# Row statistics on ACT, a split opening, a last tile in halves, and a POOL clip for ten weight tiles

## What is computed

```python
# stage 1: a gated mixer: per head, outer products of a context with itself,
# a causal convolution of 1024 taps, contracted with the normalised input
kv  = einsum('bhil,bhjl->bijhl', ctx, ctx)             # 64 heads, head_dim 8
y   = irfft(rfft(kv, 2 * L) * rfft(ssm_kernel, 2 * L))[..., :L]
out = einsum('bijhl,bhil->bjhl', y + kv * D, layernorm(x))
x   = x + tanh(g_xattn) * out
# stage 2: a gated feed-forward block with MXINT8 operands
h = bf16(layernorm(bf16(layernorm(x))) * ln_w + ln_b)
h = bf16(mx_quant(h) @ mx_quant(W1).T + b1)            # 1024 -> 4096
h = bf16(gelu_tanh(h))
h = bf16(mx_quant(h) @ mx_quant(W2).T + b2)            # 4096 -> 1024
x = x + tanh(g_ffn) * bf16(bf16(layernorm(x)) + h)
# mx_quant: blocks of 32, amax, scale = 2**floor(log2(amax)) / 64, round, clip to [-128, 127]
```

## Time and profile before

| | us |
|---|---|
| median of 3 runs | 1933.82 (1930.59 to 1935.32) |
| the profiled execution | 1932.06 |
| its span, first to last instruction | 1930.3 |
| PE busy in the span | 1854.4 (96%) |
| DVE busy | 1625.8 (84%) |
| ACT busy | 1042.8 (54%) |
| POOL busy | 880.8 (46%) |

### The profile page before, as it was taken

One profiled execution on the slowest core, in us unless ns is written; L12 is line 12 of the kernel. 1 busy time (PEld: TensorE's weight loads), 2 busy tenths in 40 slices (PEclk: granted clock), 3 DMA queues, 4 the chain that ended last, 5 costly groups with the idle time before them and its releaser, 6 DMA issues. The chain is left out here.

```text
span 1930.3 us, 28627 instructions
## 1 busy us (share of the span) xinstructions
PE 1854.4 (96%) x11432; PEld 1476.1 (76%) x11432; DVE 1625.8 (84%) x1866; ACT 1042.8 (54%) x1311; POOL 880.8 (46%) x645
## 2 busy tenths in 40 slices
PE   6999999999999989999987897999999999999998
PEld 5999889999998879998975566666667776666773
DVE  5888898989999979998859998988988888889843
ACT  5666656555668677776734345444454543444440
POOL 2888888788899889998940000000000000000000
PEclk9999999999999999999998998999999999999999
DMA  7665657777757587785758312112212212121112
GB/s 241 213 221 175 192 180 229 228 260 267 220 188 234 188 254 209 242 256 188 212 202 328 88 55 77 66 51 70 77 45 77 77 68 69 51 77 56 44 44 77
DMA packets 165477, 294.24 MB, mean 152 GB/s; under 512 B 106144, under 2 KB 106144, under 8 KB 157152
## 3 DMA queue, kind: packets, MB, share of 16 engines
q1 hardware_dynamic: 165344, 292.41, 46.9%
HBM read 222.05 MB, written 45.68 MB: 139 GB/s over the span
## 5 line engine op out<-in xcount | busy, mean ns | idle before, releaser
L372 PE MATMUL y_ps<-kk_hi,slab 128*128 128x352 f32 (+6 forms) x3328 | 882.9, 348 | 33.6 <-DMA slab<-taps_scratch 18.4
L372 PEld LDWEIGHTS y_ps<-kk_hi,slab 128*128 128x128 f32 x3328 | 598.3, 190 | 89.7 <-issue 26.2
L372 PE MATMUL y_ps<-kk_lo,slab 128*128 128x352 f32 (+6 forms) x1664 | 576.4, 346 | 0.0
L1073 PE MATMUL l_ps<-f_xq_T,w_rest 128*128 128x256 bf16 x3136 | 348.4, 273 | 7.8 <-DMA f_xq_T<-f_hq 6.3
L1073 PEld LDWEIGHTS l_ps<-f_xq_T,w_rest 128*128 128x128 bf16 x3136 | 307.3, 98 | 47.5 <-issue 6.7
L1136 ACT ACTIVATE arena<-l_ps,b_c 128x256 bf16<-128x256 f32 x496 | 207.2, 473 | 247.4 <-PE l_ps L1073 242.4
L854 POOL TENSOR_TENSOR terms<-terms 128x768 f32<-128x768 f32 x127 | 332.1, 2615 | 10.0
L372 PEld LDWEIGHTS y_ps<-kk_lo,slab 128*128 128x128 f32 x1664 | 315.5, 190 | 27.2
L1374 POOL TENSOR_TENSOR f_rstd<-f_var_eps,f_neg_half 128x1 f32<-128x1 f32 x28 | 15.3, 548 | 673.0 <-DVE f_var_eps L1194 673.0
L1091 PE MATMUL acc_ps<-raw_room,arena 128*128 128x512 bf16 x1024 | 226.2, 379 | 0.0
L1091 PE MATMUL acc_ps<-w_T,arena 128*128 128x512 bf16 x1024 | 226.2, 379 | 0.0
(11 more groups left out here) (147 smaller groups left out, 2298.3 us busy)
## 6 DMA issues: line engine op xcount, KB each, us to landing
slab<-taps_scratch SPq DMA_DIRECT2D x128, 512.0 KB, 4.9
arena<-in_w_m SPq DMA_DIRECT2D x32, 1024.0 KB, 7.0
arena<-x_scratch SPq DMA_DIRECT2D x60, 512.0 KB, 3.8
raw_room<-in_ctx_e SPq DMA_DIRECT2D x64, 384.0 KB, 3.4
arena<-in_w SPq DMA_DIRECT2D x22, 1024.0 KB, 6.9
x_tile<-in_x_t SPq DMA_DIRECT2D x32, 512.0 KB, 5.0
out_t<-arena SPq DMA_DIRECT2D x32, 512.0 KB, 2.6
w_scratch<-arena SPq DMA_DIRECT2D x22, 512.0 KB, 7.4
```

What stands on the lines that cost most here:

```text
L372: mm = nc.tensor.matmul(y_ps[:, at + begin - first:at + end - first], slab[s][:, half, d * P:(d + 1) * P], kk_part[s][:, begin - d * PAIR: ...
L1073: mm = nc.tensor.matmul(l1_ps[bank % L1_BANKS][:, a, :], w1_tile(b)[:, k, a * P:(a + 1) * P], inputs[:, k, :], start=(k == 0), stop=(k == ...
```

## The change

1. **Opening of stage 1.** The gate is loaded first and has its own semaphore. The taps are scaled straight into their high half, and the low half is one `scalar_tensor_tensor`. The two halves are stored, waited for and read back one by one; PE starts on the high half's slab and takes the low taps of the first stretch last. ACT makes `high_half(0)` ahead of the statistics of the first tile.
2. **Jobs of stage 1.** ACT clips a job between `squares` and `high_half`, no longer after `copy_k`; SP loads the next job into a slot right behind that slot's `store_job`, one head earlier than before.
3. **Order of the first banks.** `LAG` goes; group 1 uses tiles 4 and 5 at once, then one bank of group 1 for every second tile, and the last five at the end.
4. **Row statistics on ACT.** `first_statistics` and `second_statistics` leave DVE: each is two ACT passes with an accumulator (mean, then square about the mean) and a small third one. For tiles 4 to 7 they are placed among the banks and gelus of groups 1 and 2, afterwards behind `norm_again`. The second statistics use the loaded tile as scratch, so the next load waits for them instead of for `first_norm`.
5. **DVE's order** in groups 1 and 2: peaks come after the inputs, and three peaks of group 2 between its two inputs.
6. **POOL clips.** `weight_clip` of the ten tiles moves from DVE to POOL; the quantisation of the first of these tiles is not held behind the next tile's integers.
7. **Last tile in halves.** Layer 2 of tile 31 runs all of the first 512 columns, then the others; sums and store go by halves.

```diff
 # SP, stage 1 (the store of each half of the taps has its own semaphore)
-            sp.wait_ge(taps_stored, 32)
-            load_slab(0)
+            sp.wait_ge(taps_stored[0], 16)
+            load_half(0, 0)
+            sp.wait_ge(taps_stored[1], 16)
+            load_half(0, 1)
...
-                if h - 2 in quant_of and quant_of[h - 2] + 3 < JOBS - 1:
-                    load_job(quant_of[h - 2] + 3)
...
                 if h - 1 in quant_of:
                     store_job(quant_of[h - 1])
+                    if quant_of[h - 1] + 3 < JOBS - 1:
+                        load_job(quant_of[h - 1] + 3)
 # ACT, stage 1
             squares(0)
+            high_half(0)
             ln_stats(0)
-            high_half(0)
...
                     squares(h + 1)
+                    if h in quant_of:
+                        job_clip(quant_of[h])
                     high_half(h + 1)
...
-                if h in quant_of:
-                    job_clip(quant_of[h])
 # stage 2: PE's order of the first banks
-    for b in range(FILL, banks + LAG):
-        first_banks += [(0, b)] if b < banks else []
-        first_banks += [(1, b - LAG)] if b >= FILL + LAG else []
+    first_banks = [(g, b) for g in range(2) for b in range(FILL, KEPT)]
+    for b in range(KEPT, banks):
+        first_banks += [(0, b)]
+        first_banks += [(1, (b + KEPT) // 2)] if (b - KEPT) % 2 == 0 else []
+    first_banks += [(1, b) for b in range(banks) if b >= FILL and (1, b) not in first_banks]
 # stage 2, ACT (second_statistics is the same on n_bf, with xin as scratch)
+            def first_statistics(t):
+                i, u = t % GROUP, t - EARLY
+                x = xin[t % X_LOADS]
+                act.wait_ge(x1_loaded[u % X_LOADS], 16 * (u // X_LOADS + 1))
...
+                nc.scalar.activation(n_bf[i][:], x, ACT.Identity, scale=-1.0 / L, accum_out=neg_mean1[i][:]).then_inc(mean1, 1)
...
+                nc.scalar.activation(n_bf[i][:], x, ACT.Square, bias=neg_mean1[i][:], accum_out=spread1[:]).then_inc(sum1, 1)
...
+                nc.scalar.activation(var_eps1[i][:], spread1[:], ACT.Copy, scale=1.0 / L, bias=EPS).then_inc(var1, 1)
...
+                if (g, b) == (1, banks - 2):
+                    first_statistics(EARLY)
+            gelu(1, 0)
+            first_norm(EARLY)
+            gelu(1, 1)
+            second_statistics(EARLY)
+            first_statistics(EARLY + 1)
+            gelu(1, 2)
+            first_norm(EARLY + 1)
+            second_statistics(EARLY + 1)
+            gelu(1, 3)
 # stage 2, DVE
                 weight_ints(j)
-                if j > KEPT:
+                if j > KEPT + 1:
                     weight_quant(j - 1)
                 weight_scales(j)
-                weight_clip(j)
-                if j in (KEPT, 11):
-                    peak(0, 0 if j == KEPT else 1)
+                if j == KEPT:
+                    weight_quant(j)
+                if j in (8, 12):
+                    peak(0, j // 4 - 2)
 # stage 2, POOL
+            def weight_clip(j):
+                pool.wait_ge(w_scaled, j - KEPT + 1)
+                nc.gpsimd.tensor_scalar(wq[j % 2], wq[j % 2], 127.0, None, ALU.min).then_inc(ints_ready, 1)
+
+            for j in range(KEPT, W_TILES):
+                weight_clip(j)
 # stage 2, PE: the last tile's layer 2
+                if t == tiles - 1:
+                    c = part
+                    for k in range(HID // P):
+                        mm = nc.tensor.matmul(acc_ps[s][:, c * 512:(c + 1) * 512], hidden[g % 2][:, k, s * P:(s + 1) * P],
...
```

More of the change, by code:

```diff
@@ L368, in conv_stretch @@
                 deepest = (end - 1) // PAIR
-                for d in range(deepest + 1):
-                    begin = max(first, d * PAIR)
[L371 to L374, removed]
+                terms_of = ((0, kk_hi), (0, kk_lo), (1, kk_hi))
+                order = [(d, c) for d in range(deepest + 1) for c in range(3)]
+                if h == 0 and i == 0:
+                    order = [(d, c) for d, c in order if c < 2] + [(d, c) for d, c in order if c == 2]
+                for n, (d, c) in enumerate(order):
+                    half, kk_part = terms_of[c]
+                    begin = max(first, d * PAIR)
+                    if h == 0 and i == 0 and (d, c) == (0, 2):
+                        pe.wait_ge(slab_loaded[0], 16)
+                    mm = nc.tensor.matmul(y_ps[:, at + begin - first:at + end - first], slab[s][:, half, d * P:(d + 1) * P],
+                                          kk_part[s][:, begin - d * PAIR:end - d * PAIR],
+                                          start=(n == 0), stop=(n == len(order) - 1))
                 if i in (1, len(stretches) - 1):
@@ L1012, in store @@
             def store(t):
-                sp.wait_ge(out_ready, t + 1)
-                sp.dma_start(out_t[order(t)], xfin).then_inc(out_stored, 16)
+                halves = 2 if t == tiles - 1 else 1
+                for c in range(halves):
+                    part = slice(c * L // halves, (c + 1) * L // halves)
+                    sp.wait_ge(out_ready, t + 1 + c)
+                    sp.dma_start(out_t[order(t)][:, part], xfin[:, part]).then_inc(out_stored, 16)
             def load_layer2(j):
@@ L1050, in _ @@
                     reload(GROUP * (g - 1) + 1)
[L1051 removed]
+            sp.wait_ge(out_stored, 16 * (tiles + 1))
         @block.tensor
@@ L1345, in _ @@
                         quantise_input(GROUP * (g + 1) + s)
-                    if g >= 2 and s == 0:
+                    if 2 <= g <= groups and s == 0:
                         gated_sum(GROUP * (g - 2) + 1)
@@ L1350, in _ @@
                         gated_sum(0)
-                    if 1 <= g < groups:
+                    if 3 <= g < groups:
                         peak(g, s)
+                    if g == 2 and s == 0:
+                        for q in range(3):
+                            peak(g, q)
+                if g == 1:
+                    peak(g, 0)
+                    peak(g, 1)
                 if g < groups:
-                    peak(g, 2)
+                    if g != 2:
+                        peak(g, 2)
                     peak(g, 3)
@@ L1357, in _ @@
                     hidden_quantise(g)
-                for s in range(GROUP):
-                    if g + 2 < groups:
-                        first_statistics(GROUP * (g + 2) + s)
                 if 2 <= g <= groups:
@@ L1386, in _ @@
             for g in range(2, groups):
-                for i in range(GROUP):
-                    first_rstd(GROUP * g + i)
-                for i in range(GROUP):
-                    second_rstd(GROUP * g + i)
+                if g < 4:
+                    for i in range(GROUP):
+                        first_rstd(GROUP * g + i)
+                        second_rstd(GROUP * g + i)
+                else:
+                    for i in range(GROUP):
+                        first_rstd(GROUP * g + i)
+                    for i in range(GROUP):
+                        second_rstd(GROUP * g + i)
 def gated_layer(nc, x_t, ctx_e, g_x, g_f, taps_in, skip_in, ln_w, ln_b, w1_t, w2_t, w_m, b1, b2, out_t):
```

150 lines of the change are left out of this document (86 added, 64 removed).

## The result

| | before | after |
|---|---|---|
| median, us | 1932.46 (4 runs) | 1944.34 (4 runs, 1943.13 to 1944.89) |
| ratio, 95% interval | | 1.0059 [1.0042, 1.0077] |
| profiled execution: span, us | 1930.3 | 1943.1 |
| stage 2 begins (its first matmul) | 1005.05 | 994.85 |
| last weight tile quantised, Q | 1053.74 | 1076.63 |

The account below looks back on a forecast made before the run. PE was taken as the bound wherever it has work. Terms of -2.8, -9, -6 and -1.5 summed to -19.3 us on 1932.1, giving 1912.8, or 1914.5 as median against 1933.8; range 1901 to 1936.

Parts of the forecast that it names:

- Part 3: Stage 2's ten weight tiles: with the clip on POOL a tile takes 5.5 us instead of 4.08, ten of them 14 more.
- X: POOL's price for clipping one weight tile, taken as 2.0 us, with 1.8 and 4.6 kept as other values.
- Rival A: Weight tiles: POOL's clip costs as much as two inputs, 4.6 us; 1940.5 us, slower than before; chance 0.17.
- the turns: Weight tiles: POOL and DVE alternate by whole instructions, so the clip's full price is added to DVE's pace.
- rival B: Weight tiles: POOL's clip costs 3.2 us, between forecast and two-input price; +12, so 1926.5 us; chance 0.15.
- the forecast's own slope: Weight tiles: for each us by which POOL's clip price is over 2.0, add 10 us.
- Part 4: Stage 2 after the weight tiles: new order pays their delay back, net -6 us at 1202, where PE becomes full.
- Parts 1 and 2: Stage 1: earlier opening, -2.8 us (0 to -3.4); earlier job loads remove two long PE waits, -9 us (0 to -12).
- Parts 5 and 6: Steady groups of stage 2: ACT's added statistics cost 0; last tile by halves: -1.5 us (-1.2 to -2).
- Rival C: Weight tiles: POOL and DVE do not exclude each other; a tile takes 3.5 us, Q is 1047, total 1897; chance 0.05.

Follow-up runs that it names:

- experiment 5: Changed kernel plus extra instructions behind its last sums: POOL clips and products alone, then POOL's clip beside short DVE passes; POOL's clip costs 2.53 ns an element and 0.2 us.
- experiment 6: Changed kernel plus POOL-alone instructions of 1024 columns behind its last sums, in several forms; tensor_scalar by min took 2.77 us.
- experiment 3: Changed kernel with POOL clipping only the first 1024 of each weight tile's 2048 columns: 1917.16 us, ratio 0.9923 to the kernel before.
- experiment 4: Changed kernel with the quantisation of groups 1 and 2 in four parts each, clip still on POOL: 1938.60 us, ratio 1.0037 to the kernel before.
- experiment 1: Changed kernel with the clip of the ten weight tiles back on DVE: 1904.08 us, ratio 0.9853 to the kernel before.

## Why the prediction was wrong

**The step that failed is Part 3, the price X of a clip on POOL.** It was taken as 2.0 us from a row of 128 elements, with 4.6 as the upper bound from the rows with two inputs. It is 5.36, above both ends. The 128-element row is an affine select, another form; `tensor_scalar` takes 0.53 us for as many. The bound rested on a tacit assumption, that one input can't cost more than two; experiments 5 and 6 show that on POOL it does: 2.77 us for 1024 elements of bf16 against 2.12. The nearest row in size and inputs was not near in form, and the range was cut at a bound with no reason for it. Rival A (X = 4.6, chance 0.17) came nearest with 1940.5 us, 4 below the measurement. That is partly luck: its price was still 0.76 us too low, and its turn as much too long as the forecast's. Its limit, slower from X = 3.9 on, lies between the two that were run: with half a clip, 2.77 us, the kernel was faster than before (experiment 3), with 5.36 slower.

The Trainium skill (GPSIMD Engine Reference, Elementwise - side-by-side cycle accounting) gives about 2.6 cycles an element for two inputs and 1.8 as the best case; rival B used the latter. At the 1.2 GHz that the page names, two float32 inputs come to 2.17 ns x 1.2 = 2.6 cycles, as it says, two bf16 inputs to (2114 - 190) / 1024 x 1.2 = 2.3, and `tensor_scalar` to 2.53 x 1.2 = 3.0, above both figures. The measurement decides.

**In the same part, the turns were sized too long.** The exclusion is real (experiment 5), but a two-input pass of DVE is held only for the clip less 1.8 us. POOL's addition of stage 1, on which the turns were read, had held DVE to 0.15 us before its end (647.68 + 3.75 - 2.29 = 649.14 against 649.29); why the clip lets go earlier, no run shows. By the formula 2.20 + 1.27 + X a tile would take 8.83 us; it takes 6.90. At X = 5.36 the forecast's own slope, 10 us for each us of X, gives Q 44.6 us later; it came 33.1 later. The shorter turn saved 19.3 us of the 44.6. Another 7.9 us were lost where the forecast added nothing: 5.7 in the first tiles and the last one, in which DVE waits for a clip to its end, and 2.2 in the two peaks, the second of them beside a clip. So the mechanism was right, the price far too low, and the turn too long by 1.9 us a tile, which hid part of the error.

The prediction quoted a lock held for a whole instruction from the Trainium skill (SBUF - State Buffer, Who interferes with whom). These runs agree with it only in part: a two-input pass went on 1.7 us before the clip's end, and a `tensor_scalar` pass, which that section counts among those that can use DVE's two ports, was held to the end of a clip of 2048 columns (5.38 us), but not of one of 1024 (experiment 3). Whether it used two ports here, no run shows. The measurement decides.

**Part 4** had the order of events right: layer 2 begins at 1088.30, Q + 11.7 (forecast 11.5), group 2 at 1115.92, Q + 39.3 (40.5), the fourth group's stall is 4.66 us for the reload (5). It missed the stall of 6.36 at group 2. The prediction weighed DVE against POOL's clips only, not DVE's own long passes against POOL's roots, which before had taken 0.55 us in the mean of 28 and took 3.02 after. With the slow clock behind it this is 4 to 5.7 us (experiment 4) of the 9 by which this part fell short. In experiment 1 the stretch from Q to PE's end (1041.41 to 1897.62) gains 14.0 of the 17; where the other 3 are stays open.

**Parts 1 and 2 came near in size, but not in all of their steps.** PE began at 16.33, a gain of 2.0 (2.8 forecast), and waited for `kk_lo`. That was to come 1 us earlier and came at 13.67 + 2.56 = 16.23 (15.94 before): ACT's first copy waited for the context's load until 8.65 (7.58), which used up what the new order saved. So the gain is only what the slab had kept PE beyond `kk_lo`. The rest of stage 1 gained 8.2 (9). The two long waits are gone, as forecast, but waits for `kk_lo` grew. PE's waits of before at the first matmul of a head (the profile names no releaser), and DVE's waits for `kk_hi` before and after:

```profile
PE y_ps L372 <- issue: 5.9, 8, 1.4
...
DVE kk_lo L654 <- ACT kk_hi L484: 8.1, 10, 3.1
...
DVE kk_lo L670 <- ACT kk_hi L501: 20.6, 22, 2.8
```

The prediction held that ACT's clip of a job, moved ahead of `high_half`, makes `low_half` no later except where ACT is late already. But DVE's waits for `kk_hi` rose from 8.1 to 20.6 us, and PE's at the first matmul of a head from 5.9 in eight to 10.4 in fifteen. Around 846 us of the changed kernel, ACT ends `squares`, goes straight into the two passes of a clip (846.57 to 850.32) and only then casts; PE then waits 1.62 us. So PE's standing in stage 1, after its first matmul, fell by only 4.1 us, from 16.5 to 12.4. The other 4.1 are PE's pace: the same matmuls took 966.1 us instead of 970.2. Before, the granted clock was 0.50 for 3.4 us from 693.0 on and for 6.8 us from 904.6 on, at the two long waits; after, it was 1.00 throughout the stage. That the sum came out near 9 is in part luck: half of it is the clock, which the prediction had as a little.

**Parts 5 and 6 held.** The steady groups cost 0. The tail gained 2.0 (1.5).

One sum of the prediction is off. Rival C has Q at 1047 and 1897 us; by the forecast's own slope, X = 0 gives 20 us less than the forecast, so 1044.7 and 1894.5. Nothing hangs on it.

## What to carry to other kernels

An instruction that is moved to another engine is priced by the same form on that engine; where the trace has no row of it, the range must not end at the price of another form, however plausible the order of the two. Where two engines exclude each other, a pass that is moved off the busy engine can cost it more than the pass itself did: here 0.61 us of work on DVE became 3.57 us of standing still, and half the clip still cost 0.98. And when long passes are moved or lengthened on one side, look for the one-element instructions of the other that sit on a chain.

## What had not been expected of the hardware

- On POOL a `tensor_scalar` costs 2.53 ns an element, of int16, bf16 or float32: 2.77 us for 1024 of bf16, more than a `tensor_tensor` (2.11); a second operation adds 0.86 us for 1024, and a copy takes 1.04.
- Beside a clip of 5.4 us, a two-input pass on DVE lasts 3.7 us (0.28 alone), a `tensor_scalar` to the clip's end, and a pass with one input in PSUM is not held at all. Beside a clip of 2.77 us, the `tensor_scalar` was through 1.66 us before the end.
- A one-element instruction of POOL that takes 0.55 us undisturbed took 6.71 beside passes of 4.42 and 2.29 us on DVE: it got through only after the second.
